# The leaky slope of the graph convolutions split into a linear part and a floor at zero

## The reference, cut to what matters

```python
xl = (x @ Wl).reshape(n, H, D)
xr = (x @ Wr).reshape(n, H, D)
m = jax.nn.leaky_relu(xl[src] + xr[dst], NEG_SLOPE)
e = jnp.einsum('ehd,hd->eh', m, att)
e_max = jax.ops.segment_max(e, dst, num_segments=n)
ex = jnp.exp(e - e_max[dst])
denom = jax.ops.segment_sum(ex, dst, num_segments=n)
alpha = ex / (denom[dst] + 1e-16)
```

## Time and profile before

| | us |
|---|---|
| median of 2 runs | 6023.07 |
| lowest and highest run | 6015.77, 6030.36 |
| span of the profiled execution | 6037.5 |
| first `conv_logits`, first transfer to last store | 1242.4 to 1760.8 |
| second `conv_logits` | 2617.2 to 3134.9 |
| its share of the span, both together | 17% |

### The profile page before, as it was taken

One profiled execution on the slowest core, in us unless ns is written; L12 is line 12 of the kernel. 1 busy time (PEld: TensorE's weight loads), 2 busy tenths in 40 slices (PEclk: granted clock), 3 DMA queues, 4 the chain that ended last, 5 costly groups with the idle time before them and its releaser, 6 DMA issues. The chain is left out here.

```text
span 6037.5 us, 71358 instructions
## 1 busy us (share of the span) xinstructions
PE 3381.0 (56%) x13980; PEld 1953.5 (32%) x13980; DVE 3709.0 (61%) x10702; ACT 2564.7 (42%) x5746; POOL 3636.7 (60%) x3368
## 2 busy tenths in 40 slices
PE   1221674369968944469978944434445996003332
PEld 0111232223325534423334534421113774002221
DVE  2332898956668979966658969981114555982221
ACT  1222897856641246656651247771111222650100
POOL 4777343467745666667744666657772444448887
PEclk9999996589989977779988966656667998555555
DMA  7332777932214245522212257752221112983343
GB/s 244 93 93 74 234 254 284 368 99 55 55 40 158 80 148 172 173 70 55 55 45 67 79 185 245 248 197 54 54 54 46 53 54 93 341 299 63 61 64 50
DMA packets 531584, 778.51 MB, mean 129 GB/s; under 512 B 162156, under 2 KB 217736, under 8 KB 528752
## 3 DMA queue, kind: packets, MB, share of 16 engines
q1 hardware_dynamic: 427952, 620.88, 30.7%
q0 software_dynamic: 103488, 156.17, 10.8%
HBM read 475.60 MB, written 312.09 MB: 130 GB/s over the span
## 5 line engine op out<-in xcount | busy, mean ns | idle before, releaser
L919 DVE TENSOR_TENSOR conv_logits_leaky<-conv_logits_z,conv_logits_sloped 128x512 f32<-128x512 f32 x784 | 542.4, 692 | 242.9 <-ACT conv_logits_sloped L882 237.6
L1314 PE MATMUL conv_nodes_o_ps<-wmean,conv_nodes_hT 128*128 128x128 f32 x1568 | 318.9, 366 | 454.4 <-ACT conv_nodes_hT L1378 427.0
L882 ACT ACTIVATE conv_logits_sloped<-conv_logits_z 128x512 f32<-128x512 f32 x784 | 468.3, 597 | 220.9 <-PE conv_logits_z L845 119.9
L192 POOL DMA_INDIRECT AGG<-conv_aggregate_rows,conv_aggregate_idx x392 | 385.1, 982 | 261.7 <-ACT conv_aggregate_rows L1177 166.3
L186 POOL DMA_INDIRECT conv_logits_hd<-H,conv_logits_idx x392 | 372.2, 949 | 127.7 <-issue 117.9
L186 POOL DMA_INDIRECT conv_logits_hs<-H,conv_logits_idx x392 | 372.1, 949 | 119.5 <-issue 119.2
L1314 PEld LDWEIGHTS conv_nodes_o_ps<-wmean,conv_nodes_hT 128*128 128x128 f32 x1568 | 271.0, 261 | 519.9 <-ACT conv_nodes_hT L1378 458.9
L1908 PE MATMUL mean_edges_turned<-mean_edges_ident,mean_edges_hs 128*128 128x128 f32 x196 | 54.6, 434 | 685.6 <-DMA mean_edges_hs<-H,mean_edges_idx 685.6
L1286 POOL TENSOR_TENSOR conv_nodes_agg<-conv_nodes_agg,conv_nodes_bias 128x512 f32<-128x512 f32 x196 | 248.5, 1268 | 310.8 <-DVE conv_nodes_scaled L1347 146.2
L1141 PE MATMUL conv_aggregate_y<-wl,conv_aggregate_diff 128*128 128x512 f32 x784 | 393.5, 627 | 31.8 <-DVE conv_aggregate_part L1204 31.8
L246 ACT ACTIVATE conv_nodes_scaled<-conv_nodes_o,conv_nodes_norm_shift,conv_nodes_norm_rstd 128x128 f32<-128x128 f32 x784 | 322.8, 482 | 170.5 <-DVE conv_nodes_norm_shift L241 165.1
(11 more groups left out here) (241 smaller groups left out, 10015.2 us busy)
## 6 DMA issues: line engine op xcount, KB each, us to landing
conv_nodes_h<-H SPq DMA_DIRECT2D x196, 256.0 KB, 2.7
conv_nodes_agg<-AGG SPq DMA_DIRECT2D x196, 256.0 KB, 3.0
AGG<-gine_edges_zero SPq DMA_DIRECT2D x14, 1792.0 KB
gine_mlp_x<-x SPq DMA_DIRECT2D x98, 256.0 KB, 2.7
gine_mlp_agg<-AGG SPq DMA_DIRECT2D x98, 256.0 KB, 3.2
YT<-gine_mlp_yT SPq DMA_DIRECT2D x98, 256.0 KB, 3.2
gine_finish_x<-x SPq DMA_DIRECT2D x98, 256.0 KB, 3.9
gine_finish_yT<-YT SPq DMA_DIRECT2D x98, 256.0 KB, 5.0
```

What stands on the lines that cost most here:

```text
L192: return pool.indirect_dma_start(out=table, out_offset=bass.IndirectOffsetOnAxis(ap=index, axis=0), in_=rows, in_offset=None, bounds_check ...
L882: act.activation(sloped[H * j + h][:, :], z[h][:, :], ACT.Copy, scale=SLOPE).then_inc(sloped_made[j], 1)
L919: dve.tensor_tensor(leaky[H * j + h][:, :], z[h][:, :], sloped[H * j + h][:, :], ALU.max).then_inc(leaky_made[j], 1)
L1314: last = pe.matmul(o_ps[k % 2][:, a, :], hT[k % 2][:, a * P:(a + 1) * P], g.wmean[:, :], start=True, stop=True)
```

## The change

The leaky relu with slope 0.2 is written as `leaky(z) = 0.2 z + 0.8 relu(z)`. `att` is scaled by 0.8 once at the start, and the floor at zero is one operation per head, which reads PSUM and writes `above`.

- For the edges the linear part is one more product: `lin^T diffT`, where column 32 h of `lin` (128x128, the other columns zero) holds 0.2 times the sum over features of `Wl` times `att`. It starts the accumulation in `dots[1]`, and the four products with `att` are added onto it. Only `diffT` enters. The part of the edge's argument that comes from `hdT` alone is the same for all edges and the self loop of one `dst`, so it falls out of the softmax.
- For the self loops no linear part is added for the same reason: `dot_self` has the four products alone.
- Who does the floor: for self loops ACT for all 4 heads; for edges ACT for head 0 and DVE for heads 1 to 3. Before, each of the 8 took an ACT and a DVE operation.
- The phase's start gains a broadcast load of `att` as a row (128x512), a product, a reduction and two scalings on DVE, and one memset.

```diff
+                broadcast_rows(sp, att_rows[:, :], g.att_rows[layer], weights_in)
...
-                        past(pe, leaky_made[1], H * (n - 1) + h + 1)
+                        past(pe, edges_made if h else edge_made, (H - 1) * (n - 1) + h if h else n)
...
-                        pe.wait_ge(leaky_made[0], H * n + h + 1)
+                        pe.wait_ge(self_made, H * n + h + 1)
...
-                def dot(j):
-                    def step(k, i):
-                        n = i * K + k
-                        pe.wait_ge(leaky_made[j], H * n + H)
-                        past(pe, logit_made[j], n)
-                        for h in range(H):
-                            last = pe.matmul(dots[j][32 * h:32 * h + 32, :], att[:, h, :], leaky[H * j + h][:, :],
-                                             start=True, stop=True, tile_position=(0, 32 * h))
-                        last.then_inc(dots_done[j], 1)
-                    return step
-
-                pipeline(pe, nb, K, [(1, z_self), (2, dot(1)), (0, turn), (1, z_edge), (1, dot(0))])
+                def dot_self(k, i):
+                    n = i * K + k
+                    pe.wait_ge(self_made, H * n + H)
+                    past(pe, logit_made[0], n)
+                    for h in range(H):
+                        last = pe.matmul(dots[0][32 * h:32 * h + 32, :], att[:, h, :], above[h][:, :],
+                                         start=True, stop=True, tile_position=(0, 32 * h))
+                    last.then_inc(dots_done[0], 1)
+
+                def dot_edge(k, i):
+                    n = i * K + k
+                    past(pe, logit_made[1], n)
+                    pe.matmul(dots[1][:, :], lin[:, :, :], g.diffT[:, bass.ds(n * TILE, TILE)], start=True, stop=True)
+                    pe.wait_ge(edge_made, n + 1)
+                    pe.wait_ge(edges_made, (H - 1) * n + H - 1)
+                    for h in range(H):
+                        last = pe.matmul(dots[1][32 * h:32 * h + 32, :], att[:, h, :], above[H + h][:, :],
+                                         start=False, stop=True, tile_position=(0, 32 * h), skip_group_check=True)
+                    last.then_inc(dots_done[1], 1)
+
+                pipeline(pe, nb, K, [(1, z_self), (2, dot_edge), (0, turn), (1, z_edge), (1, dot_self)])
...
-                            act.activation(sloped[H * j + h][:, :], z[h][:, :], ACT.Copy, scale=SLOPE).then_inc(sloped_made[j], 1)
...
+                        act.wait_ge(z_done[0], H * n + h + 1)
+                        act.activation(above[h][:, :], z[h][:, :], ACT.Relu).then_inc(self_made, 1)
...
+                    act.wait_ge(z_done[1], H * n + 1)
+                    act.activation(above[H][:, :], z[0][:, :], ACT.Relu).then_inc(edge_made, 1)
...
-                pipeline(act, nb, K, [(1, slope(0)), (2, copy_dots(1)), (0, copy_dst), (1, slope(1)), (1, copy_dots(0))])
+                pipeline(act, nb, K, [(1, relu_self), (2, copy_dots(1)), (0, copy_dst), (1, relu_edge), (1, copy_dots(0))])
...
+                dve.memset(lin[:, :, :], 0.0)
                 dve.memset(att[:, :, :], 0.0).then_inc(att_set, 1)
-                dve.wait_ge(weights_in, 48)
+                dve.wait_ge(weights_in, 64)
+                heads = att_rows[:, :].rearrange("p (h d) -> p h d", h=H)
+                dve.tensor_tensor(att_rows[:, :], att_rows[:, :], g.wl[:, :], ALU.mult).then_inc(lin_step, 1)
+                dve.wait_ge(lin_step, 1)
+                dve.tensor_reduce(out=slopes[:, :], in_=heads, axis=AX.X, op=ALU.add).then_inc(lin_step, 1)
+                dve.wait_ge(lin_step, 2)
+                dve.tensor_scalar(lin[:, :, 0], slopes[:, :], SLOPE, None, ALU.mult)
+                dve.tensor_scalar(att[:, :, :], att[:, :, :], 1.0 - SLOPE, None, ALU.mult)
...
-                            dve.tensor_tensor(leaky[H * j + h][:, :], z[h][:, :], sloped[H * j + h][:, :],
-                                              ALU.max).then_inc(leaky_made[j], 1)
...
-                pipeline(dve, nb, K, [(1, leak(0)), (0, diff), (1, leak(1))])
+                def relu_edges(k, i):
+                    n = i * K + k
+                    past(dve, dots_done[1], n)
+                    for h in range(1, H):
+                        dve.wait_ge(z_done[1], H * n + h + 1)
+                        dve.tensor_scalar(above[H + h][:, :], z[h][:, :], 0.0, None, ALU.max).then_inc(edges_made, 1)
+
+                pipeline(dve, nb, K, [(0, diff), (1, relu_edges)])
```

## The result

The changed kernel takes 6114.34 us (median of 2 runs, 6111.20 to 6117.49) against 6023.07 us, a ratio of 1.0148 with a 95% interval of 1.0113 to 1.0183. It is 1.5% slower, inside the 2% that was called "the same". The forecast was 6108 us, with 6088 to 6132 as its range.

A forecast was written before the change was run, and what follows sets the result against it. The prediction took PE's own pace as the bound. Per convolution 41.3 + 1.0 + 0.5, twice, made 85.6 us, 85 after 0.4 us of lost gather time now covered; 6023 + 85 = 6108 us, range 6088 to 6132.

The forecast's parts named there:

- PE's own pace bounds the tile, POOL is a close second: In `conv_logits`, PE sets the tile at about 10.08 us; POOL's gathers need 9.99 to 10.08.
- The race in the earlier trace: Second convolution before the change: PE falls 4.5 us behind POOL's gathers over the stage, so PE sets the pace.
- The product costs 0.86 us a tile: `lin^T diffT` on PE, priced like a `z` product: 0.86 us a tile, 41.3 us per convolution.
- ACT and DVE give nothing back: Operations taken off ACT and DVE in each tile gain nothing; both had 3.5 us or more spare.
- The new waits cost nothing: Relus waiting for earlier `att` products, and edge heads queued behind `diff` on DVE, cost PE nothing.
- The start, 1.0 us per convolution: At the phase's start, one more 128x512 transfer ahead of `att` and the indices on SP costs 1.0 us per convolution.
- The end, +0.5 us: At a convolution's end, `lin` stands between the last self group and the last edge products: +0.5 us.
- POOL and SP: POOL gets slack of 0.9 us a tile and towards the end waits for SP's late index loads; no cost.
- Hidden product: Rival: PE has at least 0.86 us of slack a tile, POOL's gathers bound; time 6023 us; chance 0.05.
- Time back from DVE: Rival: `z_self` loads' 21.3 us put down to `leaky` is a true wait the change removes; 6064 us; chance 0.05.
- The `att` products one after another: Rival: adding onto a full product's bank serializes the `att` group, +2.58 us a tile, 6361 us; chance 0.07, milder form included.
- Table loads: Rival: alternating Relu and Copy on ACT loads a table each time, 6206 us or above; chance 0.02.

The follow-up runs named there:

- e9: Kernel before with POOL issuing 4 gathers a tile and not 8; 10.09 us a tile in both convolutions, 6020.7 us, ratio 0.9964.
- e8: Changed kernel without its product, the edges' `z` products over 128 of 512 columns; 10.08 and 10.00 us a tile, 6028.4 us, ratio to before 1.0008.
- e10: Changed kernel without its product, with short `z_edge` products and half the gathers; 7.55 us a tile, 5779.9 us, ratio to before 0.9569.
- e7: Changed kernel with adjacent `att` groups and four 128-column products replacing the full one; 10.09 and 10.00 us a tile, 6037.3 us, ratio to before 0.9999.
- e2: Kernel before plus one full product whose result is overwritten; 10.94 us a tile, 6110.3 us, ratio 1.0133.
- e3: Changed kernel with its added product issued twice; 11.80 us a tile, 6206.6 us, ratio to the kernel before 1.0297.
- e4: Changed kernel with the added product over 256 of 512 columns, same two weight loads; 10.51 us a tile, 6074.6 us, ratio to before 1.0060.
- e1: Changed kernel without its added product; 10.09 and 10.08 us a tile, 6034.0 us, ratio to the kernel before 1.0007.
- e5: Changed kernel with the self loops' `att` group moved next to the edges'; 10.60 us a tile, 6083.1 us, ratio to before 1.0080.

## Why the prediction was right, point by point

- **PE's own pace bounds the tile, POOL is a close second.** Right. With half the gathers PE still needs 10.08 us (e9), so the bound is its own; with less PE work the gathers hold the tile at 10.08 and 10.00 (e8), so they stand right behind; with both, it falls by 2.5 us (e10). The race in the earlier trace rows had told it in one convolution. What spoke most for the other side in the first one, 42 waits of `turn` for gathers, 37.8 us, the prediction didn't look at; the gaps of 0.84 us under e7 show them to be no waits but for 2.2 us ahead of tile 1 (a gap of 3.04) and 0.4 in all after it. In the first, where both need 10.08 us, the 47 tiles grew by 39.9 us and in the second by 40.3, so the closeness of POOL changed nothing.
- **The product costs 0.86 us a tile.** Right to 0.01 us: 10.94 - 10.09 = 0.85 and 10.94 - 10.08 = 0.86. e2, e3 and e4 give the same price alone, twice and for half the columns. The upper bound of 1.00 wasn't needed.
- **ACT and DVE give nothing back.** Right, by e1 (without the product, the tile of before) and e2 (with it and the old work on ACT and DVE, the tile of the changed kernel). The floor on DVE was assumed at 730 ns and takes 692, which changes nothing here.
- **The new waits cost nothing.** Right: no wait of PE for ACT or DVE stands between `turn` and `turn`, and the tiles are 10.94 us apart.
- **The start, 1.0 us per convolution.** From the phase's start to the first `turn` it was 16.8 us and is 17.6 in the first convolution, +0.8. In the second it grows by about 1.0.
- **The end, +0.5 us.** It is 2.05 - 1.48 = +0.57.
- **POOL and SP.** The late indices came as told, and cost nothing. e3 makes it plainer. There POOL's idle time ahead of the `hd` gathers is 202.1 us where the changed kernel has 136.2 (the page's groups), and the tile grows by the product only.
- **The sum.** 85 us by rows, +42.3 and +42.7 in the two phases. For the first the parts add up to that: 0.8 at the start, 39.9 in the 47 tiles, 0.86 for the 48th product in the loop, 0.57 at the end, 42.1 in all. The median moved by 91, and the 6 us between the two are within what runs of one kernel differ by. That the total came within 6 us of 6108 is partly luck: the forecast stands on the median of two runs of the kernel before, 6023, and its median in the three later sets was 6030 to 6037. The phases are the measure of the sum.
- **The rivals.** *Hidden product:* it fell with e2. The Trainium skill ("Perfetto Trace Analysis", section Identifying the Most-Contended Engine) judges TensorE's headroom by two measures, its arithmetic as a share of the peak and the busy share of its weight loads, and calls matmul busy time a bad measure; the prediction took up the second. That share is 40% before, 40% in the changed kernel and 40% in e9 (139.57 of 350.00), all with PE as the bound, and it is 39% in e8 (174.85 of 450.00), where the gathers bind. In this phase it doesn't tell the two apart, while PE's matmul busy share does (100% in the first three, 80% in e8), and the measurement decides. *Time back from DVE:* the 21.3 us put down to `leaky` were no wait. In the changed kernel `leaky` is gone, and the step from `z_self`'s first load to its third is 2905.18 - 2904.64 = 0.54 us, now with the releaser "issue". *The `att` products one after another:* the group still takes 0.99 us. *Table loads:* none in the phase.

## What to carry to other kernels

An operation taken off two engines is a gain only where one of them sets the pace, so the first thing to find for such a trade is which engine's starts are evenly spaced without a wait, and whether the work is moved onto it. Here a tile lost 8 of its 20 operations on ACT and DVE (11 and 9 became 8 and 4) for one product on the engine that had no idle time, and the price was that product's columns. Where two engines have nearly the same pace, the lag between them over the whole stage tells which one leads, and how little is to be won by speeding up that one alone. And a wait that the profile names is only as long as its gap goes beyond the gap that stands at the same place without it.

## What was not expected of the hardware

- A passage from full-array products to 32-column products and back costs 0.34 us here (e5 against the changed kernel, 10.94 to 10.60 us a tile), of which 0.14 is in the `att` groups and 0.19 where `z_edge` and `z_self` now follow each other. The earlier trace rows had shown only parts of it.
- Four products of 128 columns, one in each group of 32 columns, take 0.22 us together, a quarter of one full product over 512 columns (0.86). The parts of the result then lie on different partitions, and no run here prices what it takes to join them.
- The clock granted to PE was 0.95 on the mean of the stretch in e8 in which PE waited for each gather, where it was 1.00 (the 2.4 GHz level) in every stretch shown with PE full.
